# Wo stage of an attention and mixture-of-experts kernel: order of VectorE's steps, two steps on GpSimd, and two buffers in the experts

## The reference

```
out = softmax(q @ k.T * scale, causal) @ v          # per head; x is [2048, 512]
x1  = layernorm(x + out @ Wo + bo)                  # the Wo stage
logits = x1 @ router_weight.T                       # [2048, 64]
topw, topi = top_k(softmax(logits), 8); topw /= sum(topw)
pos = running count of tokens per expert - 1        # a token is kept where pos < 256
for each expert e:  xe = the tokens placed in e     # up to 256 rows
    g, u = split(xe @ gate_up[e]);  ye = (silu(g) * u) @ down[e]
y = sum over a token's experts of topw * ye
result = layernorm(x1 + y)
```

## Time and profile before

| | |
|---|---|
| time, median of 3 runs (lowest, highest) | 2180.68 us (2179.51, 2182.07) |
| the profiled execution's own time | 2180.33 us |
| its span, first to last instruction | 2178.5 us |
| TensorE busy | 2044.0 us (94%) |
| VectorE, ScalarE, GpSimd busy | 1675.8 (77%), 1361.8 (63%), 814.9 us (37%) |
| mean granted TensorE clock | 0.975 |

### The profile page before, as it was taken

How to read it: one execution, slowest core, us unless ns; L and a number is a source line. 1 busy time by engine, 2 the same in 40 slices (tenths; PEclk the granted TensorE clock), 3 DMA queues, 4 the chain that set the end, 5 groups by cost and what they waited for, 6 DMA issues and landing times. The chain is left out here.

```text
span 2178.5 us, 41238 instructions
## 1 busy us (share of the span) xinstructions
PE 2044.0 (94%) x13409; PEld 1808.9 (83%) x13409; DVE 1675.8 (77%) x3503; ACT 1361.8 (63%) x2735; POOL 814.9 (37%) x792
## 2 busy tenths in 40 slices
PE   8999989999999999999999999899959999999990
PEld 6888878988888988899888898677748999999980
DVE  5899987877678776787767876577757888888874
ACT  3677776766667656676666766322327777877761
POOL 1000023332233322332323332133335777787760
PEclk9999999999999999999999999999969999999995
DMA  7558563010520105201062000767637999999987
GB/s 243 184 216 286 215 217 123 34 59 21 183 104 26 59 22 189 98 25 63 18 238 87 25 26 20 264 239 275 232 102 217 296 297 299 303 293 296 298 220 245
DMA packets 140170, 362.60 MB, mean 166 GB/s; under 512 B 16209, under 2 KB 33233, under 8 KB 135377
## 3 DMA queue, kind: packets, MB, share of 16 engines
q1 hardware_dynamic: 111312, 292.09, 37.7%
q0 software_dynamic: 28672, 68.17, 13.2%
HBM read 224.27 MB, written 135.94 MB: 165 GB/s over the span
## 5 line engine op out<-in xcount | busy, mean ns | idle before, releaser
L653 PE MATMUL p_S<-p_kT,p_q 128*128 128x512 f32 (+3 forms) x1920 | 473.6, 377 | 10.6 <-ACT p_prob L729 9.9
L653 PEld LDWEIGHTS p_S<-p_kT,p_q 128*128 128x128 f32 x1920 | 324.2, 190 | 59.0 <-ACT p_prob L729 15.3
L840 POOL TENSOR_SCALAR p_prob<-p_prob,p_inv 128x128 f32<-128x128 f32 (+7 forms) x256 | 191.3, 747 | 457.1 <-DVE p_inv L789 457.1
L840 POOL TENSOR_SCALAR p_prob<-p_prob,p_inv,p_part 128x1024 f32<-128x1024 f32 x128 | 153.0, 1196 | 496.0 <-DVE p_inv L794 496.0
L665 PE MATMUL p_TP<-p_ident,p_prob 128*128 128x128 f32 x2176 | 304.4, 274 | 1.8 <-DVE p_pT1l L800 1.8
L778 DVE TENSOR_REDUCE p_nmax<-p_S 128x1 f32<-128x1024 f32 (+7 forms) x256 | 251.7, 983 | 23.0 <-PE p_S L653 22.0
L665 PEld LDWEIGHTS p_TP<-p_ident,p_prob 128*128 128x128 f32 x2176 | 246.2, 141 | 25.9 <-DVE p_pT1l L800 5.6
L738 ACT CAST p_pT1h<-p_TP 128x512 fp32r<-128x512 f32 (+3 forms) x320 | 154.7, 526 | 152.9 <-PE p_TP L665 152.7
L738 ACT CAST p_pT0h<-p_TP 128x512 fp32r<-128x512 f32 (+3 forms) x320 | 155.2, 526 | 151.9 <-PE p_TP L665 150.6
L686 PE MATMUL p_O<-p_pT0h,p_v 128*128 128x256 f32 x1088 | 227.5, 293 | 6.0 <-DVE p_pT0l L800 6.0
L686 PE MATMUL p_O<-p_pT1h,p_v 128*128 128x256 f32 x1088 | 226.7, 293 | 6.2 <-issue 3.8
(11 more groups left out here) (221 smaller groups left out, 4507.4 us busy)
## 6 DMA issues: line engine op xcount, KB each, us to landing
p_w_raw<-in_gu SPq DMA_DIRECT2D x64, 768.0 KB, 6.9
qk_scratch<-p_qout SPq DMA_DIRECT2D x80, 512.0 KB, 2.7
p_q<-qk_scratch SPq DMA_DIRECT2D x16, 2048.0 KB, 9.2
o_scratch<-p_oT SPq DMA_DIRECT2D x128, 256.0 KB, 2.3
p_ot<-o_scratch SPq DMA_DIRECT2D x32, 1024.0 KB, 7.0
p_w_raw<-in_gu SPq DMA_DIRECT2D x64, 256.0 KB, 8.3
v_scratch<-p_vout SPq DMA_DIRECT2D x16, 512.0 KB, 3.2
p_t_raw<-in_dn SPq DMA_DIRECT2D x32, 256.0 KB, 7.9
```

The source lines that it names most:

```text
L653: mm = nc.tensor.matmul(out, x, y, start=(n == 0), stop=(n == 2))
L840: nc.gpsimd.tensor_scalar(prob[k][:, cols], prob[k][:, cols], inv[:, k:k + 1], scale, ALU.mult, ALU.mult).then_inc(normed, 1)
```

## The change

In the Wo stage:

- VectorE's order in step b becomes normalise(b), place(b-1), choose(b), mark(b-1). The last steps are written out in the same order, with `weights_lo` between place and choose.
- `residual` (x plus bias) moves to GpSimd.
- TensorE's `TURN` goes from 7 to 6 and `ROUTE` from 9 to 8. `TABLE` (12) and `SUM` (14) stay.
- For block 14 VectorE makes four of the eight `hi_hot` rows and GpSimd the other four, ahead of all eight `lo_hot` rows. For block 15 GpSimd makes five `lo_hot` rows, and VectorE the other three and all of `hi_hot`.

In the experts `xT` gets a second buffer (`turn_hi(e)` waits for gate_up(e-2)), and expert 1's transposes stand between the first and the second part of gate_up(0).

```
         PARTS = 4
+        DVE_HIS, POOL_LOS = 4, 5
...
-            TURN, ROUTE, TABLE, SUM = 7, 9, 12, 14
+            TURN, ROUTE, TABLE, SUM = 6, 8, 12, 14
...
-            def residual(b, k, n):
-
-                dve.wait_ge(xr_in[k], n * 16 + 16)
-                nc.vector.tensor_tensor(xb[k][:], xr[k][:], bo_b[:], ALU.add).then_inc(biased, 1)
...
-                link(nc.vector.tensor_scalar(number[:], number[:], float(P), None, ALU.add))
                 if not early:
                     dve.wait_ge(lo_ready, b)
+                link(nc.vector.tensor_scalar(number[:], number[:], float(P), None, ALU.add))
...
-            def mark(b, early):
+            def mark(b, early=False, his=range(TOPK), los=()):
 
                 dve.wait_ge(placed, b + 1)
                 if not early:
                     dve.wait_ge(tabled, b)
-                for n in range(TOPK):
+                for n in los:
+                    nc.vector.tensor_scalar(lo_hot[:, n, :], iota_lo[:], lo[:, n:n + 1], None, ALU.is_equal)
+                for n in his:
                     ins = nc.vector.tensor_scalar(hi_hot[:, n, :], iota_lo[:], hi[:, n:n + 1], number[:], ALU.is_equal,
                                                   ALU.mult)
                 ins.then_inc(hi_ready, 1)
 
-            def step(i, first, last=False, end=False):
+            def step(i, first, last=False):
                 for k in range(2):
                     b = i * 2 + k
-                    after = not (first and k == 0)
-                    if after:
+                    normalise(b, k, i, first)
+                    if not (first and k == 0):
                         place(b - 1, 1 - k, first)
-                    normalise(b, k, i, first)
-                    if not (end and k == 1):
-                        residual(b + 1, 1 - k, i + k)
-                    if after:
-                        mark(b - 1, first)
                     if last:
                         weights_lo(dve, b)
                     choose(b, k, i, first)
+                    if not (first and k == 0):
+                        mark(b - 1, first)
...
-            step(NB // 2 - 1, False, last=True, end=True)
+            normalise(NB - 2, 0, NB // 2 - 1, False)
+            place(NB - 3, 1, False)
+            weights_lo(dve, NB - 2)
+            choose(NB - 2, 0, NB // 2 - 1, False)
+            mark(NB - 3)
+            normalise(NB - 1, 1, NB // 2 - 1, False)
+            place(NB - 2, 0, False)
+            mark(NB - 2, his=range(DVE_HIS))
+            choose(NB - 1, 1, NB // 2 - 1, False)
             place(NB - 1, 1, False)
-            mark(NB - 1, False)
+            mark(NB - 1, los=range(POOL_LOS, TOPK))
...
+            def residual(b, k, n, early):
+
+                wait_alone(pool, passed, xr_in[k], n * 16 + 16)
+                if not early:
+                    wait_alone(pool, passed, normed, b - 1)
+                nc.gpsimd.tensor_tensor(xb[k][:], xr[k][:], bo_b[:], ALU.add).then_inc(biased, 1)
+
+            def mark(b, early, los=range(TOPK), his=()):
+
+                wait_alone(pool, passed, placed, b + 1)
+                if not early:
+                    wait_alone(pool, passed, tabled, b)
+                for n in his:
+                    nc.gpsimd.tensor_scalar(hi_hot[:, n, :], iota_lo[:], hi[:, n:n + 1], number[:], ALU.is_equal, ALU.mult)
+                for n in los:
+                    ins = nc.gpsimd.tensor_scalar(lo_hot[:, n, :], iota_lo[:], lo[:, n:n + 1], None, ALU.is_equal)
+                ins.then_inc(lo_ready, 1)
...
+                residual(i * 2 + 1, 1, i, first)
+                mark(i * 2, first)
+                residual(i * 2 + 2, 0, i + 1, False)
+                mark(i * 2 + 1, False)
...
+            mark(NB - 2, False, his=range(DVE_HIS, TOPK))
+            mark(NB - 1, False, los=range(POOL_LOS))
...
-        xT = [sb(f"xT{s}", [P, NC, CAP], F32R, kb=1 + 4 * (s == "l")) for s in "hl"]
+        xT = [[sb(f"xT{k}{s}", [P, NC, CAP], F32R, kb=(1, 130)[k] + 4 * (s == "l")) for s in "hl"] for k in (1, 0)][::-1]
...
             turn(0)
-            gate_up(0)
+            gate_up(0, range(1))
             turn(1)
+            gate_up(0, range(1, 3))
...
-                    if e >= 1:
-                        act.wait_ge(gated, e)
-                    nc.scalar.copy(xT[HI][:, :, c * P:(c + 1) * P], tp[c][:]).then_inc(x_hi, 1)
+                    if e >= 2:
+                        act.wait_ge(gated, e - 1)
+                    nc.scalar.copy(xT[e % 2][HI][:, :, c * P:(c + 1) * P], tp[c][:]).then_inc(x_hi, 1)
```

More of the change, by code:

```diff
@@ L1028, in project @@
                         mm = nc.tensor.matmul(acc[k][:], a, w, start=(n == 0 and m == 0), stop=(n == H - 1 and m == 2))
-                if n == H - 1:
+                if heads and heads[-1] == H - 1:
                     mm.then_inc(projected, 1)
@@ L1236, in step @@
                     choose(b, k, i, first)
-            residual(0, 0, 0)
+                    if not (first and k == 0):
+                        mark(b - 1, first)
             step(0, True)
@@ L1259, in gpsimd @@
                            allow_small_or_imprecise_dtypes=True).then_inc(iota_ready, 1)
-            def step(i, first):
-                for k in range(2):
-                    b = i * 2 + k
-                    wait_alone(pool, passed, placed, b + 1)
-                    if not (first and k == 0):
-                        wait_alone(pool, passed, tabled, b)
-                    for n in range(TOPK):
-                        ins = nc.gpsimd.tensor_scalar(lo_hot[:, n, :], iota_lo[:], lo[:, n:n + 1], None, ALU.is_equal)
-                    ins.then_inc(lo_ready, 1)
-            loop(pool, NB // 2, step)
+            pool.wait_ge(const_in, 64)
+            def residual(b, k, n, early):
[12 more added lines that the diff above has]
+                ins.then_inc(lo_ready, 1)
+            def step(i, first):
+                residual(i * 2 + 1, 1, i, first)
+                mark(i * 2, first)
+                residual(i * 2 + 2, 0, i + 1, False)
+                mark(i * 2 + 1, False)
+            residual(0, 0, 0, True)
+            step(0, True)
+            with pool.Fori(1, NB // 2 - 1) as i:
+                step(i, False)
+            residual(NB - 1, 1, NB // 2 - 1, False)
+            mark(NB - 2, False, his=range(DVE_HIS, TOPK))
+            mark(NB - 1, False, los=range(POOL_LOS))
     return Programs(sync, tensor, scalar, vector, gpsimd)
@@ L1388, in turn, with gate_up @@
                     mm.then_inc(turned, 1)
-            def gate_up(e):
+            def gate_up(e, fs=range(3)):
                 k = e % 2
@@ L1395, in gate_up @@
                     pe.wait_ge(h_rest, e)
-                for f, out in enumerate((pgu[:, 0, :], pgu[:, 1, :], prest[:])):
-                    for m, (a, b) in enumerate(split3(w_s[k], xT)):
+                for f in fs:
+                    out = (pgu[:, 0, :], pgu[:, 1, :], prest[:])[f]
+                    for m, (a, b) in enumerate(split3(w_s[k], xT[k])):
                         for d in range(NC):
@@ L1401, in gate_up @@
                                                   stop=(m == 2 and d == NC - 1))
-                mm.then_inc(gated, 1)
+                if fs[-1] == 2:
+                    mm.then_inc(gated, 1)
             def down(e):
@@ L1556, in turn_lo @@
                     cols = slice(c * P, (c + 1) * P)
-                    nc.vector.tensor_tensor(xT[LO][:, :, cols], tp[c][:], xT[HI][:, :, cols].bitcast(F32), ALU.subtract
+                    nc.vector.tensor_tensor(xT[e % 2][LO][:, :, cols], tp[c][:], xT[e % 2][HI][:, :, cols].bitcast(F32), ALU.subtract
                                             ).then_inc(x_lo, 1)
```

## The result

The changed kernel took 2268.97 us (median of 4 runs, 2265.1 to 2270.76) against 2180.73 for the kernel before. The ratio is 1.04, interval 1.0386 to 1.0414: 88 us slower. The forecast was 2240, with 2253 as its upper end, so it was wrong by 29 us, though direction and place were right. The profiled execution took 2270.76 us, its span is 2268.9, and its mean TensorE clock 0.958 (0.975 before).

A forecast was written before the change was run, and what follows sets the result against it. TensorE was taken to bound the Wo stage. Loop stall, weights, tail (two terms), experts and clock, 41.5 + 4 - 1.35 + 2.4 - 3.5 + 17 = +60, on 2180.3 gave 2240 us, range 2218 to 2253.

The forecast's parts named there:

- 3.35 plus the weights' 4 / 14: Wo loop: TensorE's table waits about 3.35 us a block for mark; splitting experts' weights adds 4 us in all.
- the sum over VectorE's four steps: Wo loop: normalise, place, choose and mark take 12.0 us by their rows, so mark ends at 13.15.
- Splitting the weights: Wo blocks 13, 14 and 15: splitting the experts' weights now stands in the loop ahead of choose, +4 us.
- mark(b-1): 2.3 us: Last VectorE step of a Wo block: takes 2.3 us, to 13.15, while the table is due at 9.8.
- Cost zero at either end: Wo stage: the residual on GpSimd takes 0.65 to 2.6 us, ends before its 17.0 deadline, costs nothing.
- holding up as a rival: Wo loop: `hot` waits for one GpSimd row, up to 0.65 in 14 blocks: +9, 2249 us; chance 0.08.
- The row I trusted: Earlier trace, Wo stage: `residual` took 0.68 us during GpSimd's rows, no longer than neighbours at 0.69, so no hold-up expected.
- I take 1.2 a block: Wo stage: low TensorE clock after each wait costs 1.2 us a block, x 14, +17 us.
- The rival with the clock up: Wo stage: the stall comes but TensorE's clock stays up, 2223 us; chance 0.2.
- some 18 with falls: Expected sign in the Wo stage: counts 16.6 us apart at full clock, some 18 with clock falls.
- I take -3.5: Experts' start: second buffer lets SiLU start 2.0 us earlier, perhaps sparing a clock fall; -3.5 us, bounds 2.0 and 3.5.
- The tail, +1.05 forecast: End of Wo stage: -1.35 us from last counts to block 15's `h`, +2.4 from there to first gather.

The follow-up runs named there:

- e1: The changed kernel with the residual (x plus bias) back on VectorE, behind mark: 2253.19 us, ratio 1.0338.
- e5: The changed kernel with each table three heads into the following block, block 13's table in the tail: 2181.74 us, ratio 1.0002.
- e4: The changed kernel with mark(b-1) ahead of choose(b) again, behind place: 2229.57 us, ratio 1.0227.
- e3: The changed kernel with 18 matmuls of 512 columns, never read, ahead of the table in each block: 2241.81 us, ratio 1.0276.
- e7: The kernel before with the experts' part of the change alone (second xT buffer, expert 1's transposes ahead): 2179.79 us, ratio 0.9995.
- e8: e6 plus a one-column SiLU, never read, behind the copies of expert 1's rows, to load its table early: 2175.22 us, ratio 0.9974.
- e6: e5 with all eight `hi_hot` rows of block 14 made on VectorE, none on GpSimd: 2177.8 us, ratio 0.9986.
- e2: The changed kernel with GpSimd's sum of x and bias done twice, once into a spare tile: 2280.91 us, ratio 1.0458.

## Why the prediction was wrong

**Right: the order, and where it stalls.** TensorE waits for `hi_hot` 14 times, the transposes don't wait in the loop, the table of block 14 waits for GpSimd. With the residual on VectorE (e1) the wait is 49.2 / 14 = 3.5 us, against 3.35 plus the weights' 4 / 14, together 3.64. So the sum over VectorE's four steps was good to 0.15 us, and e5 confirms that the table's place behind them carries the loss. Splitting the weights was put at 4 us; by the longer waits of the last three blocks (5.22, 5.55 and 6.09 against 4.38) it cost 3.7.

**Wrong: "mark(b-1): 2.3 us", and the residual's "Cost zero at either end".** I bounded how long the sum would take on GpSimd (0.65 to 2.6; it took 1.25) and looked whether it would be late. I did not ask what it would do to VectorE while it ran. It begins right behind the eight rows of `lo_hot`, and that is when mark runs. Mark grew to between 3.07 and 3.36 us, inside the loop through both engines: 4.6 us of wait instead of 3.64, 13.5 us over 14 blocks by the profile, 16 by e1. I had weighed holding up as a rival, but for the wrong pair: `hot` under a `lo_hot` row. That pair indeed costs next to nothing, 0.69 to 0.72; that the rival's 2249 is the nearest of the list is luck. `hot` under the sum does get held, 1.61 us once in e4. The row I trusted, `residual` under `lo_hot`, showed one kind of work on GpSimd, and the change put another kind there. The Trainium skill (SBUF — State Buffer, "Who interferes with whom") does list VectorE's `tensor_scalar`, which is mark's kind, among those that may take the port pair shared with GpSimd when they run in a mode with two ports, with the other engine blocked for a whole instruction. No run here shows in which mode mark ran. The 1.29 beside 1.25 agrees. Under `lo_hot` rows of 0.65 the same instruction took at most 0.40 before and up to 0.75 in the changed kernel, and most of them took at most 0.40 there too, which that rule doesn't explain.

**Wrong in size: "I take 1.2 a block", the clock.** It was 2.1: 29.65 us by the profile and 29.9 by e3, not 17. I had counted with the 3.3 us of low clock near 811.7 in the earlier trace rows, and there it was indeed no longer, as the next stretch of the kernel before shows:

```profile
815.00:818.00 3.00, 3.00 (x25) 2.63 (x23) 1.81 (x5) 1.50 (x4) 1.63 (x2) 0.98 0.00 0
```

In the two blocks shown above it lasted 6.8 us, and so it did behind twelve of the 14 waits. The length behind one pause did not carry over to another, longer one. So everything from the table to the next block's first heads ran at half speed, and from the table to `h` took 5.84 us instead of the 3.63 of e3. The rival with the clock up was far off. With both terms too small the counts stood 20 us apart, not "some 18 with falls".

**Wrong in size: the experts, "I take -3.5".** It was -0.9 here, and nothing that could be told in e7. I put all 2.0 us ahead of SiLU down to the copies; 1.28 of them were its table load, which the change doesn't touch (e7, e8). The pause was 2.76 us instead of the 1.4 of the forecast, and the clock still fell behind it, though not behind the same pause in e7.

**The tail, +1.05 forecast, +1.8 measured.** GpSimd's `hi_hot` rows (two operations each) take 0.82 us, not the 0.59 to 0.65 of a `lo_hot` row. That sharing out block 14's rows loses was right, and e6 shows it in the late order.

Together: 26.2 us too little in the loop (13.5 for mark and what goes with it, 12.65 for the clock), 2.6 for the experts, 0.8 for the tail and 0.8 at the start make 30.3, the whole miss against the profiled execution. The range was too narrow above because its upper end held one hold-up of 9 us and no clock price over 17: two costs that can come together were bounded one at a time.

**Open.** Why GpSimd's sum of two tiles of 512 columns holds an instruction of VectorE each time, by its whole length for mark's rows, while a row of `lo_hot` holds one only now and then and for less. The sum differs from a row in its kind and in its length, and no run changes one of the two alone. Also what sets the length of the low clock. It went with the length of the pause: eleven falls of 3.4 us and one of 6.8 behind pauses of 1.9 to 3.5 us (e4), eight and six behind pauses of mostly 3.1 to 3.5 us (e1), two and twelve behind 4.1 us and more (the changed kernel), none shorter than 6.8 behind 5.3 us and more (e2).

## What to carry to other kernels

An instruction moved to an idle engine is costed three times: how long it takes there, when it is wanted, and what runs on the neighbouring engine meanwhile; the last is read from rows with the same kinds on both sides, or it has no price yet. Where two engines wait for each other in a loop, a stall of the one is paid again as clock: after pauses of 4 us some 7 us ran at half speed in twelve cases of 14, and filling the pause with useless matmuls gained 27 us. And before a step is moved ahead of another, the order of its consumer goes with it: here one table moved to the next block gave back 87 of the 88 us.
